# Macaron block with a state-space middle phase: a unit's sixteen half-width products in one run, in two banks of their own

## The reference

```python
proj = h @ W_in.T                       # z, x, B, C, dt
xBC  = silu(causal_conv4(xBC) + conv_b)
x_dt = x * dt                           # 64 heads of width 64
Y_diag = einsum('bclhn,bcshn,bhcls,bcshp->bclhp', C, B, L, x_dt)   # within a chunk
states = einsum('bclhn,bhcl,bclhp->bchpn', B, decay_states, x_dt)  # what a chunk adds
new    = prev * exp(d_k) + s_k          # the state carried from chunk to chunk, first prev = 0
Y_off  = einsum('bclhn,bhcpn,bhcl->bclhp', C, prev_states, exp(A_cum))
y = Y_diag + Y_off + D * x;  g = y * silu(z)
out = (rms_norm(g) * norm_w) @ W_out.T
```

## Time and profile before

| what | us |
|---|---|
| median of three runs | 2496.81 |
| lowest, highest | 2495.47, 2498.77 |
| span of the profiled execution | 2493.7 |
| PE busy in it | 2278.8 |
| DVE, ACT, POOL busy | 1725.5, 1437.7, 1474.0 |
| first slot that begins with L2072 behind L2039, to the last of the first sequence | 449.9 to 1220.5 |
| the same in the second sequence | 1333.0 to 2096.0 |

### The profile page before, as it was taken

The page is one execution under the profiler, slowest core; times in us unless marked ns, Lnnn a source line. Parts: engine busy times, 40 slices in busy tenths (PEclk is TensorE's granted clock), DMA queues, the critical chain, the costliest instruction groups (busy, mean ns, idle before and its releaser), DMA issues. The chain is left out here.

```text
span 2493.7 us, 44179 instructions
## 1 busy us (share of the span) xinstructions
PE 2278.8 (91%) x11910; PEld 1779.2 (71%) x11910; DVE 1725.5 (69%) x3562; ACT 1437.7 (58%) x2899; POOL 1474.0 (59%) x1306
## 2 busy tenths in 40 slices
PE   5799977999999999999888999999999998579997
PEld 3677765777777777777566777777777776358776
DVE  6432276788887878788877788878878787653226
ACT  5133326676676766776556776667767775413332
POOL 2876342666666666666426666666666665178533
PEclk8999989999999999999899999999999999689999
DMA  8665342332333334334213333343333332165545
GB/s 334 236 190 161 125 143 60 89 89 89 94 105 86 86 92 105 88 88 97 66 41 95 89 88 97 97 96 88 88 93 101 84 88 51 52 232 187 161 134 192
DMA packets 204905, 285.33 MB, mean 114 GB/s; under 512 B 16288, under 2 KB 148458, under 8 KB 204816
## 3 DMA queue, kind: packets, MB, share of 16 engines
q1 hardware_dynamic: 185936, 219.18, 31.6%
q0 software_dynamic: 18880, 65.02, 8.4%
HBM read 225.43 MB, written 58.72 MB: 114 GB/s over the span
## 5 line engine op out<-in xcount | busy, mean ns | idle before, releaser
L1306 POOL TENSOR_TENSOR mamba_mix<-mamba_mix,mamba_scores 128x512 f32<-128x512 f32 x256 | 330.8, 1292 | 272.8 <-ACT mamba_mix L1490 272.8
L1989 PE MATMUL mamba_p_proj<-mamba_xt_lo,mamba_in_hi 128*128 128x512 f32 x1056 | 462.2, 438 | 7.0 <-DVE mamba_xs L1683 5.2
L1990 PE MATMUL mamba_p_proj<-mamba_xt_hi,mamba_in_hi 128*128 128x512 f32 x1056 | 415.9, 394 | 0.0
L1991 PE MATMUL mamba_p_proj<-mamba_xt_hi,mamba_in_lo 128*128 128x512 f32 x1056 | 415.5, 394 | 0.0
L1486 ACT ACTIVATE mamba_mix<-mamba_cum_l,mamba_cum_g 128x128 f32<-128x128 f32 x1024 | 324.4, 389 | 0.6 <-issue 0.6
L1678 DVE SCALAR_TENSOR_TENSOR mamba_xs<-mamba_p_proj,mamba_taps,mamba_xs 128x511 f32<-128x511 f32 (+2 forms) x384 | 285.4, 743 | 36.3 <-ACT mamba_xs L1420 27.2
L1709 DVE TENSOR_TENSOR mamba_total<-mamba_p_out,mamba_total 128x512 f32<-128x512 f32 x256 | 177.0, 692 | 147.9 <-PE mamba_p_out L2025 143.3
L1300 POOL TENSOR_TENSOR mamba_xend<-mamba_xdt,mamba_to_end_g 128x512 f32<-128x512 f32 x128 | 160.8, 1257 | 198.8 <-DVE mamba_xdt L1736 198.8
L660 DVE TENSOR_TENSOR ffn_h<-ffn_p_gu,ffn_sil 128x256 f32<-128x256 f32 x110 | 46.9, 426 | 295.6 <-ACT ffn_sil L545 295.3
L1989 PEld LDWEIGHTS mamba_p_proj<-mamba_xt_lo,mamba_in_hi 128*128 128x128 f32 x1056 | 200.8, 190 | 62.2 <-issue 9.4
L1991 PEld LDWEIGHTS mamba_p_proj<-mamba_xt_hi,mamba_in_lo 128*128 128x128 f32 x1056 | 199.7, 189 | 45.0
(11 more groups left out here) (335 smaller groups left out, 5466.6 us busy)
## 6 DMA issues: line engine op xcount, KB each, us to landing
mamba_cum_l<-mamba_cum_rows SPq DMA_DIRECT2D x128, 512.0 KB, 5.9
mamba_rise<-mamba_exp_rows SPq DMA_DIRECT2D x256, 128.0 KB, 5.4
ffn_xs<-slots_in SPq DMA_DIRECT2D x78, 256.0 KB, 2.7
slots_out<-ffn_y SPq DMA_DIRECT2D x78, 256.0 KB, 2.4
mamba_raw_x<-in_t SPq DMA_DIRECT2D x34, 512.0 KB, 7.3
mamba_raw_z<-in_t SPq DMA_DIRECT2D x32, 512.0 KB, 8.0
mamba_raw_out<-out_t SPq DMA_DIRECT2D x32, 512.0 KB, 3.7
slots_out<-ffn_xs SPq DMA_DIRECT2D x1, 9984.0 KB, 41.9
```

What stands on the lines that cost most here:

```text
L1306: pool.tensor_tensor(mix[:, c % 2, :, :], mix[:, c % 2, :, :], scores[:, b * CPB + c, :].unsqueeze(1).broadcast_to([P, GH, P]), ALU.mult). ...
L1989: pe.matmul(bank, in_hi[:, piece, kk, :], xt_lo[:, kk, c], start=(kk == 0), stop=False)
L1990: pe.matmul(bank, in_hi[:, piece, kk, :], xt_hi[:, kk, c], start=False, stop=False)
L1991: last = pe.matmul(bank, in_lo[:, piece, kk, :], xt_hi[:, kk, c], start=False, stop=(kk == KT - 1))
```

## The change

What it does, part by part:

- PE: `recur` is split. `off(c)` (the product with the state) and `start(c)` (the chunk's own state) stay where they were. The sixteen diagonal products of the unit, `diag(0)` and `diag(1)`, run in one go after projection x0, into two banks of their own (`p_diag`), and need all four chunks of `mix` by then. The off-diagonal result moves to the free half of the bank `p_st` (`p_off`), which is not doubled: `off(c)` waits for the carry of the chunk before.
- Terms that are zero or never read go: `off` and its carry for the first chunk of a group, the memset of the state, and `start` and the state for a group's last chunk.
- ACT and POOL: `mix` has four places in place of two, and all four chunks are made for the next unit, one slot ahead. ACT's order is new; POOL's is too: the low parts of the weights stand together at the front, `decayed` of a unit's first chunk is made in the slot before.
- DVE: `carry_of(0)` and `next_state(0)` come before `gate`; the three taps of a tile run together; D*x is one instruction per tile of 512 columns (`add_skip`) in place of eight of 128, and `add_carry` is two of 384 or 512 columns in place of four of 256; `stage` is split in two.
- SP: the second `cum_l` half is loaded for both units at the loop body's end, behind the fourth `Exp` of a slot.
- In each sequence's first slot `diag(1)` stands behind z0, and ACT makes chunks 2 and 3 there.

The core of the diff:

```diff
-        mix = sb("mix", [P, 2, GH, P])
-        carry = sb("carry", [P, 2, CT, P])
+        mix = sb("mix", [P, CPB, GH, P])
+        carry = sb("carry", [P, CT, BLK])
...
-        p_y = ps("p_y", [P, 2, 2, CT, P])
+        p_diag = ps("p_diag", [P, CT, BLK])
+        p_off = p_st[:, GC:2 * GC].rearrange("p (h l) -> p h l", h=CT)
...
+                def off(c):
+
+                    if (b, c) == (0, 0):
+                        return
                     s = (b * CPB + c) * P
+                    pe.wait_ge(s_state, carried(k, gi, b, c))
+                    if k > 0 or not (first and c == 1):
+                        pe.wait_ge(s_car, carried(k, gi, b, c) - 1)
...
+                def diag(j):
+
+                    pe.wait_ge(s_mix, U * CPB + 2 * j + 2)
+                    pe.wait_ge(s_xdt, U * 2 + j + 1)
+                    if j == 0 and not first:
+                        pe.wait_ge(s_y, U * CT)
+                    for c in (2 * j, 2 * j + 1):
+                        for h in range(GH):
+                            rows_of = slice(h % 2 * HD, (h % 2 + 1) * HD)
+                            mm = pe.matmul(p_diag[rows_of, h // 2, c * P:(c + 1) * P], xdt[:, c, h, :], mix[:, c, h, :],
+                                           start=True, stop=True)
+                    mm.then_inc(s_diag, 1)
...
-                recur(0)
+                off(0)
+                start(0)
                 if not last:
                     project_x(k, gn, bn, 0)
-                recur(1)
+                diag(0)
+                if not first:
+                    diag(1)
+                off(1)
+                start(1)
```

DVE's slot, the lines that change in it:

```diff
+                carry_of(0)
+                next_state(0)
                 if not first:
                     gate(k, gp, bp)
-                combine(0)
...
+                if b == 1 and not last:
+                    stage_cum(k, gn)
+                next_rows(0, 1)
+                next_stats(0)
+                conv(0, (1, 2, 3))
+                carry_of(1)
+                next_state(1)
                 if not first:
                     gate_low(U - 1, gp, 1 - b)
...
+                add_skip(0)
+                carry_of(2)
+                next_state(2)
...
+                conv(1, (1, 2, 3))
...
+                add_skip(1)
+                carry_of(3)
+                next_state(3)
+                for ct in range(CT):
+                    add_carry(ct)
```

POOL's slot and ACT's slot:

```diff
+                decay_x(k, gi, b, 1, first)
+                decay_state(k, gi, b, 1)
...
                 next_z(0)
-                decay_x(k, gi, b, 1, first)
-                decay_state(1)
                 next_z(1)
...
+                this_out(0)
+                this_out(1)
...
+                decay_state(k, gi, b, 2)
+                next_scores(0)
+                if not first:
+                    add_squares(U - 1, 1 - b, 0, second)
+                next_scores(1)
+                if b == 0:
+                    decay_state(k, gi, b, 3)
...
+                if not last:
+                    exponents(k, gn, bn, 0)
+                if b == 0 and not last_group:
+                    round_x(k, gi, V, 0)
+                if not last:
+                    exponents(k, gn, bn, 1)
+                    tap_x(k, gn, bn, 1, first)
```

More of the change, by code:

```diff
@@ L1489, in exponents @@
                 act.wait_ge(s_relu, U * CPB + c + 1)
[L1490 removed]
+                act.activation(mix[:, c, :, :], mix[:, c, :, :], ACT.Exp, scale=-1.0).then_inc(s_exp, 1)
             def dt_copy(k, b):
@@ L1538, in slot @@
                         square(U - 1, 1 - b, ct)
-                if b == 1:
-                    for ct in range(CT):
-                        round_out(k, gi, U, ct, k == 0 and second)
-                elif not last_group:
-                    round_x(k, gi, V, 0)
                 if not last:
-                    tap_x(k, gn, bn, 1, first)
-                exponents(k, gi, b, 3)
+                    exponents(k, gn, bn, 2)
                 if more:
@@ L1765, in combine, with next_state @@
-                    done.then_inc(s_y, 1)
-                def add_carry(c):
-                    n = U * CPB + c
-                    cols = slice(c * P, (c + 1) * P)
-                    dve.wait_ge(s_car, n + 1)
-                    dve.wait_ge(s_y, n + 1)
-                    dve.tensor_tensor(xs[:, b, :, cols], xs[:, b, :, cols], carry[:, c % 2, :, :],
+                def next_state(c):
+                    if (b, c) == (NB - 1, CPB - 1):
+                        return
+                    ends = p_st[:, 0:GC].rearrange("p (h d) -> p h d", h=GH)
+                    dve.wait_ge(s_st, U * CPB + c + 1)
+                    if (b, c) == (0, 0):
+                        dve.tensor_copy(state[:, :, :], ends).then_inc(s_state, 1)
+                    else:
+                        dve.wait_ge(s_decayed, faded(k, gi, b, c))
+                        dve.tensor_tensor(state[:, :, :], ends, decayed[:, :, :], ALU.add).then_inc(s_state, 1)
@@ new lines, in add_skip, with add_carry @@
+                def add_skip(ct):
+                    dve.wait_ge(s_diag, U * 2 + 2)
+                    dve.scalar_tensor_tensor(xs[:, b, ct, :], xs[:, b, ct, :], skip[:, bass.ds(gi * CT + ct, 1)],
+                                             p_diag[:, ct, :], ALU.mult, ALU.add).then_inc(s_y, 1)
+                def add_carry(ct):
+                    lo = (1 - b) * P
+                    dve.wait_ge(s_car, carried(k, gi, b, CPB - 1))
+                    dve.wait_ge(s_y, U * CT + ct + 1)
+                    dve.tensor_tensor(xs[:, b, ct, lo:BLK], xs[:, b, ct, lo:BLK], carry[:, ct, lo:BLK],
@@ L2090, in next_columns @@
                         lns.transposes(pe, k + 1, tiles)
-                recur(0)
+                off(0)
+                start(0)
                 if not last:
                     project_x(k, gn, bn, 0)
-                recur(1)
+                diag(0)
+                if not first:
+                    diag(1)
+                off(1)
+                start(1)
                 if not last:
                     project_x(k, gn, bn, 1)
-                if last:
+                else:
                     next_columns(0, 1)
                     project_out(k, gp, bp, (0,))
-                recur(2)
+                off(2)
+                start(2)
                 if last:
@@ L2106, in slot @@
                     project_z(k, gn, bn, 0)
-                recur(3)
+                if first:
+                    diag(1)
+                off(3)
+                start(3)
                 if last:
```

208 lines of the change are left out of this document (93 added, 115 removed).

## The result

The changed kernel takes 2403.57 us (median of 4 runs, 2400.51 to 2403.97) against 2497.1 us: ratio 0.9623 [0.961, 0.9637], 93.5 us less. The prediction was 2416 within 2374 to 2458, and faster. The profiled execution spans 2401.9 us.

A forecast was written before the change was run, and what follows sets the result against it. PE was taken to bound a slot for 95%, the recurrence's round trip the rest. Pair 45.5 + 0.6 + 1.8 = 48.0 against 50.71; 30 pairs save 81 us: span 2412.7, plus 3.1 gives 2416, range 2374 to 2458.

The forecast's parts named there:

- The sum's own lower bound: Good end of the open prices: no `halo` waits, z1 late by 1.2 a pair, pair 46.7, 120 us less: 2377.
- PE without waits: PE in the middle phase, never kept waiting: slots of 22.75 (b=0) and 22.8 (b=1), a pair 45.5, 5.2 less.
- upper bound of 2.17: Sixteen `diag` products in one run: 1.78 plus edges priced at 0.2 to 0.4; the upper value taken, 2.17 us.
- The sum by that rule alone: Width changes draining PE's array, 0.37 us each: 1.1 us saved a slot, the whole some 65 us shorter.
- z1 late: PE's second projection z1 waits for DVE's convolution: 1.8 us with b=0, 0.6 with b=1.
- `halo` walk: Second tile's taps, b=0: three small DVE instructions wait 0.3, 0.5 and 1.0 us for POOL operations, 1.8 in all.
- The pair: Two middle-phase slots after the change: 45.5 + 0.6 + 1.8 = 48.0 us against 50.71, 2.7 less.
- no gain at the ends of a sequence: First and last slots of each sequence have other neighbours; no gain taken, 60 of 64 slots counted as 30 pairs.
- No wait for the state, `mix` or weights: State and `mix` reach PE in time; weights land near 6.0, ACT asks at 6.4. Late-weights rival: 2455 or 2485, chance 0.07.
- The terms that go: Unread products left out on PE: `off(0)` with b=0, 0.44 us, and `start(3)` with b=1, 0.43.
- PE alone bounding the slot: Rival: meetings fall well and z1 is never late; pair 45.5, 156 us less: 2341. Chance 0.11 with values up to the range.
- POOL did take DVE's turn: Rival: POOL delays DVE's two-SBUF-operand instructions each time; pair 53.7, 2587; change loses from stalls of 5.2 a pair. Chance 0.05.

The follow-up runs named there:

- both kernels with three runs: Sixteen half-width products split into runs of 8, 8 and 16 passes, in the changed kernel (0.9692 of before) and with POOL's b=0 squares also moved late (0.9553).
- squares-late kernel: Changed kernel with POOL adding the squares only after the second tile's last tap in b=0 slots; 0.9442 of before.
- the cut there: Kernel before with the two unread groups of products cut to 2 columns each; 0.998 of before.
- late-squares kernels: Changed kernel with b=0 squares after the second tile's last tap: alone 0.9442, with first tile's D*x late in both slots 0.9425, in b=1 alone 0.9445.
- the last kernel: Against the squares-late kernel, add_skip(0) moved behind the second convolution in b=1 slots alone; 0.9445 of before.

## Why the prediction was right

The forecast's mechanism and nearly all its terms held. The total came out 12.4 us shorter than 2416: about half of that is a pair of slots that gained 2.9 and not 2.7, and most of the rest a term that was set to zero, the ends of a sequence. (The sum's own lower bound is 2377; the range states 2374.)

- **PE without waits.** Predicted 45.55 a pair. By starts: 24.85 - 1.75 + 22.94 - 0.73 = 45.31. The run of sixteen took 2.09 with its edges, where the upper bound of 2.17 was taken. The price of a width change, 0.37 from the earlier trace rows, came out at 0.35 in both kernels with three runs. What the Trainium skill says of the tiling mode in "TensorEngine Tiling (Array Packing)", Key Properties, agrees with that. The sum by that rule alone, 65 us, is too small against 93.5; with the 0.87 a pair of the terms that go, 26 us in 30 pairs, it would be 91.
- **z1 late.** Predicted 1.8 with b=0 and 0.6 with b=1; measured 1.75 (1.92 in the second sequence) and 0.73, each released by the instruction named: L1706 and L1701. The `halo` walk laid three meetings at 0.3, 0.5 and 1.0; they were 0.31, 0.46 and 1.00 (0.52, 0.67 and 1.21 less 0.21). The squares-late kernel shows that this is the cause and not a coincidence. Counted from a slot's own start (813.23, 837.62, 861.01) the slots are 24.4 and 23.4, where 24.6 and 23.4 were forecast. That the meetings fell as laid out had some luck in it: the prediction itself called them its weakest term.
- **The pair.** 48.0 predicted, 47.95 measured. Before, I had read 50.71 from one pair; the mean is 50.86 in either sequence, as b=0 slots vary from 24.9 to 25.9 in both and the one that I read, 25.10, is among the shorter. The 28 pairs give 81.4, where I had 30 x 2.7 = 81: that these agree is luck, 2.9 for 2.7 against 28 for 30.
- **The mis-sized term: no gain at the ends of a sequence.** It was put at 0. Between the sequences 6.8 us went, and behind the last x0 4.8, less 1.1 ahead of the first: 10.5 of the 12.4 us (the slots give 0.4 more, and the median lies 1.7 above the span, not 3.1). Of the 64 slots 56 lie in the 28 pairs and eight in these stretches; four pairs at 2.9 would be 11.6, so they gained about like the others. Counted the forecast's way, 30 pairs at 2.9 are 87, 6 more than its 81, and some 5 are left for the four slots that it gave nothing. That the slots in these stretches are where the time went is only argued; no run takes them alone.
- **No wait for the state, `mix` or weights.** Right, save one wait for a state in seven pairs. The weights were issued 1.4 to 1.5 us ahead of the slot (1.7 predicted) and landed 6.7 to 7.6 later, and in the steady slots ACT never waited for them (14 times and 18.1 us in the first sequence before). By the prediction's own numbers, 7.3 less 1.7, they would land at 5.6 and not "near 6.0".
- **The terms that go.** Counted at 0.87 a pair of PE's work, which is right as PE's work, and worth 0.3 to 0.46 in the changed kernel, where z1's lateness hides `start(3)`. For the kernel before no run says it, as the cut there took off only some 0.3 of the 0.87.
- **The rivals.** PE alone bounding the slot (2341) is what the late-squares kernels approach, 46.2 to 46.6 a pair against 45.3. POOL did take DVE's turn, but only where the walk had placed it; the 5.2 us a pair from which the change would lose were 2.48. What the Trainium skill says of the exclusive lock in "SBUF — State Buffer", "SBUF: two separate sides", agrees with the rows: each small instruction ended only when a POOL operation had ended, 0.07 us after the next had started.

Where the 2.9 us a pair come from can be read in two ways. By PE's queue: its work fell from 48.4 a pair (2 x 24.2) to 45.3, so by 3.1, of which the terms are 0.87 and six width changes at 0.35 to 0.37 are 2.1 to 2.2; its stalls were 2.4 before and are 2.5 now (0.2 more in the second sequence). So what was gained is PE's work, and the new orders on the other engines did no more than keep the stalls, now nearly all at z1, from growing. By experiments on either side: the order of DVE's queue 0.1 to 0.6, the terms 0.3 to 0.46, two of the three width changes removed in each slot 0.9 (48.83 against 47.95). The rest, some 1 to 1.6, belongs to the third width change, DVE's larger pieces, the new orders of ACT and POOL, the decays made a slot ahead and the banks of their own, which weren't taken apart; the kernel before can't run the sixteen products in one go without the last two. These prices needn't add up, as each is cut by z1's lateness in its own kernel.

## What to carry to other kernels

Read lateness from starts on the waiting engine, not from the idle time in brackets: 1.49 was 1.75 and 0.12 was 0.40. When two in-order queues are laid beside each other, look for the smallest instructions on the path that must wait for another engine's long operation; moving that operation behind them gave 1.4 us a pair, half of what the whole change had given. An edit that is to price a piece of work must be read for how much it took off: cutting two products to 2 columns took off 0.3 us, not 0.87. And an instruction whose wait hides an edit today may itself be released, by another way, by the engine that you edit: a wait is cover only for what isn't at its root.

## What the runs showed of the hardware

- A DVE instruction over 1 to 3 columns with two operands from SBUF takes 0.21 us with POOL idle and up to 1.22 beside a POOL operation, and in the slot shown ends 0.07 us after POOL's next one starts.
- It works both ways: `decayed` on POOL takes 0.62 beside the convolution's taps, 0.92 beside `add_carry` and 1.05 beside `gate` or `gate_low`; `mix` takes 1.29 beside the taps and 1.74 beside `gate_low`. Two `add_carry` on DVE took 2.36, 3.14 or 3.23.
- Going from full to half width and back costs 0.35 us with 4 half-width products between and 0.37 in the kernel before, also with 4; the run of sixteen, 2.09 in all, has 0.09 and 0.11 at its edges.
- Two passes of a 256-column product cut to 2 columns took 0.2 us less (0.56 for 0.77 to the second product behind them), four passes of a 128-column product 0.1 less (0.44 for 0.54).
- In one slot of the changed kernel 512-column products came 0.43 us apart and not 0.23, with a granted clock of 0.66 from 1328 to 1333 us against 1.00 in the rest of both rows of slots.
- The phases outside the middle took 894.6 us in the changed kernel's profile, 906.5 in that of squares late and 922.5 in that of the last kernel, with the same work in them and a granted clock of 0.93, 0.93 and 0.92 over the first 490 us; between 59 and 110 us it was 0.90 in the second and 0.83 in the third.
